# Mamba block: the residual rows added on TensorE with the identity, copied out by ScalarE

## The reference, cut to what matters

```
xz = einsum('bld,ed->ble', layernorm(x), in_proj_w)       # 256 -> 2 x 512: x part and gate z
u  = silu(causal_conv(x part))                            # 4 taps per channel
B, C, dt = split(u @ x_proj_w.T);  delta = softplus(dt @ dt_proj_w.T + dt_proj_b)
h_t = exp(delta_t * A) * h_{t-1} + delta_t * u_t * B_t    # 512 channels x 16 states
y   = (sum over states of h * C + D * u) * silu(z)
x   = x + y @ out_proj_w.T                                # out projection and residual
```

## Time and profile before

| | |
|---|---|
| Median of 3 runs | 3361.07 us (3359.82 to 3366.82) |
| Profiled execution, its own time | 3362.63 us |
| Its span, first to last instruction | 3360.8 us |
| Busy over the span | TensorE 2712.3 (81%), VectorE 2302.4 (69%), GpSimd 2124.2 (63%), ScalarE 1717.8 (51%) |
| Mean granted clock of TensorE | 0.906 |
| Mamba stage | from 0 to some 1815 us |

### The profile page before, as it was taken

One profiled execution on the slowest core, in us unless ns is written; L12 is line 12 of the kernel. 1 busy time (PEld: TensorE's weight loads), 2 busy tenths in 40 slices (PEclk: granted clock), 3 DMA queues, 4 the chain that ended last, 5 costly groups with the idle time before them and its releaser, 6 DMA issues.

```text
span 3360.8 us, 54089 instructions
## 1 busy us (share of the span) xinstructions
PE 2712.3 (81%) x20202; PEld 1495.0 (44%) x20202; DVE 2302.4 (69%) x2483; ACT 1717.8 (51%) x3115; POOL 2124.2 (63%) x1317
## 2 busy tenths in 40 slices
PE   5787788887888778887754499996999999359998
PEld 2233334333343333343332266554666666235665
DVE  1799999999999999999996522213666666552211
ACT  3677777777777777777751122223444443122221
POOL 1899999999999999999992054433333232124442
PEclk9899999988999889998876699998999999679999
DMA  3456565565566655666542033332111111213442
GB/s 112 103 127 155 137 144 133 140 145 140 140 138 146 146 134 132 144 149 143 133 107 60 13 90 71 83 51 59 46 46 40 52 46 38 67 28 87 89 89 25
DMA packets 227392, 330.01 MB, mean 98 GB/s; under 512 B 40546, under 2 KB 116834, under 8 KB 227011
## 3 DMA queue, kind: packets, MB, share of 16 engines
q1 hardware_dynamic: 202562, 292.49, 35.3%
q0 software_dynamic: 24576, 34.10, 6.0%
HBM read 240.52 MB, written 85.98 MB: 97 GB/s over the span
## 4 chain that ended last, share of the span: by engine, by line
PE 40%; POOL 24%; DVE 23%; issue 8%; ACT 3%; DMA 1%; SPq 0%; DVEq 0%; POOLq 0%; ACTq 0%
POOL m_side L584 14%; DVE m_pair L668 8%; POOL m_hc L593 7%; PE g_h L1341 6%; PE f_h L1341 6%; PE t_wb L2056 6%; DVE m_hc L668 5%; PE f_yp L1355 3%; PE m_wk L771 3%; PE g_yp L1355 3%; DVE m_hc L677 2%; PE t_num L2056 2%; PE m_y L863 2%; PE m_pair L919 2%; DVE t_am L1978 2%
## 5 line engine op out<-in xcount | busy, mean ns | idle before, releaser
L584 POOL TENSOR_TENSOR m_side<-m_du_r,m_bc 128x1024 f32<-128x1024 f32 x416 | 975.0, 2368 | 13.4 <-DMA m_du_r<-ddd 13.1
L351 ACT ACTIVATE m_pair<-m_delta_r,m_a_neg 128x512 f32<-128x512 f32 x832 | 539.7, 681 | 179.0 <-DVE m_hc L677 128.6
L593 POOL TENSOR_TENSOR m_hc<-m_hc,m_bc 128x1024 f32<-128x1024 f32 x208 | 492.2, 2370 | 99.6 <-DVE m_hc L668 97.9
L668 DVE TENSOR_TENSOR_SCAN m_pair<-m_pair,m_side 128x1024 f32<-128x1024 f32 x240 | 547.9, 2283 | 3.4 <-ACT m_pair L351 2.8
L863 PE MATMUL m_y<-m_hc,m_fold 128*32 128x512 f32 x2048 | 321.5, 702 | 229.8 <-DVE m_hc L677 121.2
L668 DVE TENSOR_TENSOR_SCAN m_hc<-m_pair,m_side 128x1024 f32<-128x1024 f32 x176 | 397.7, 2275 | 28.6 <-ACT m_pair L351 28.6
L677 DVE TENSOR_TENSOR m_hc<-m_pair,m_bc 128x1024 f32<-128x1024 f32 x304 | 370.5, 1219 | 7.3
L771 PE MATMUL m_wk<-m_xnT,m_w_in 128*128 128x512 f32 x512 | 276.9, 668 | 10.8 <-DVE m_cw_diag L725 10.0
L771 PE MATMUL m_wk<-m_xs,m_cw_diag 128*128 128x512 f32 x512 | 244.1, 605 | 15.5 <-ACT m_xs L416 15.5
L919 PE MATMUL m_pair<-m_b_diag,m_du_t 128*32 128x128 f32 x6144 | 203.8, 289 | 43.5 <-DVE m_hc L668 24.3
L919 PEld LDWEIGHTS m_pair<-m_b_diag,m_du_t 128*32 128x32 f32 x6144 | 179.0, 117 | 124.7 <-issue 123.4
(11 more groups left out here) (308 smaller groups left out, 4887.4 us busy)
## 6 DMA issues: line engine op xcount, KB each, us to landing
m_delta_r<-ddd SPq DMA_DIRECT2D x256, 256.0 KB, 6.8
m_du_r<-ddd SPq DMA_DIRECT2D x256, 256.0 KB, 7.7
m_bc<-bcd SPq DMA_DIRECT2D x256, 128.0 KB, 2.9
ddd<-m_delta SPq DMA_DIRECT2D x32, 512.0 KB, 3.2
ddd<-m_du SPq DMA_DIRECT2D x32, 512.0 KB, 4.1
f_w<-in_w SPq DMA_DIRECT2D x24, 512.0 KB, 6.1
g_w<-in_w SPq DMA_DIRECT2D x24, 512.0 KB, 6.1
m_xt<-in_x SPq DMA_DIRECT2D x16, 512.0 KB, 10.9
```

Of the source, the lines that this page charges most:

```text
L351: last = nc.scalar.activation(to, delta_r[:, c % 2, q, :], ACT.Exp, scale=a_neg[:, c * NQ + q, st:st + 1])
L584: nc.gpsimd.tensor_tensor(side[:, un % RING, :, :], du_r[:, c % 2, 2 * h:2 * h + 2, :], bc[:, 0, st:st + 1, :].to_broadcast([P, 2, T]), AL ...
L593: nc.gpsimd.tensor_tensor(hc[:, un % RING, :, :], hc[:, un % RING, :, :], bc[:, 1, st:st + 1, :].to_broadcast([P, 2, T]), ALU.mult).then_i ...
L668: nc.vector.tensor_tensor_scan(to, decay, added, 0.0, ALU.mult, ALU.add).then_inc(S["scan"], 1)
```

## The change

The two residual additions on VectorE are gone. TensorE adds the residual rows in the bank itself: behind the four matmuls of each 128 tokens it issues a fifth, with the identity as the stationary matrix and the loaded rows `xr` as the moving one, into the same accumulation; it waits for the load of these rows. ScalarE copies each half from the bank into `x1t` (the new `x1_out`, in its units 10 and 11, behind the fourth `cv_out` and ahead of the Silus). VectorE's statistics move from units 9 and 10 to 11 and 12, the aggregations from 10 to 12.

```diff
 # ScalarE
+            def x1_out(b, half):
+                act.wait_ge(S["op"], b * 2 + half + 1)
+                two = slice(half * 2, half * 2 + 2)
+                nc.scalar.copy(x1t[:, two, :], wk[:, half, :].rearrange("p (j c) -> p j c", c=C)).then_inc(S["x1"], 1)
...
                     if un == 7:
                         dut_out(b, 2)
+                    if post and un in (10, 11):
+                        x1_out(b - 1, (10, 11).index(un))
                     if un == 11:
                         if prep:
                             silu_u(b + 1, 1 - par)
...
             def epilogue():
+                x1_out(NB - 1, 0)
+                x1_out(NB - 1, 1)
                 out_norm3(NB - 1, 0)
 # VectorE
-            def residual(b, half):
-                dve.wait_ge(S["op"], b * 2 + half + 1)
-                if half == 0:
-                    dve.wait_ge(S["ld_xr"], b * 16 + 16)
-                two = slice(half * 2, half * 2 + 2)
-                nc.vector.tensor_tensor(x1t[:, two, :], wk[:, half, :].rearrange("p (j c) -> p j c", c=C), xr[:, two, :],
-                                        ALU.add).then_inc(S["x1"], 1)
...
-                        if un in (8, 10):
-                            residual(b - 1, (8, 10).index(un))
-                        if un in (9, 10):
-                            out_norm1(b - 1, (9, 10).index(un))
-                        if un == 10:
+                        if un in (11, 12):
+                            out_norm1(b - 1, (11, 12).index(un))
+                        if un == 12:
                             out_norm2(b - 1)
...
                 for half in range(2):
-                    residual(NB - 1, half)
                     out_norm1(NB - 1, half)
 # TensorE, outp
+                wait_alone(pe, S["ld_xr"], b * 16 + 16, S["tick"])
                 for jj in range(2):
                     j = half * 2 + jj
                     for k in range(KD):
-                        last = mm(wk[:, half, jj * C:(jj + 1) * C], yg[:, k, j * P:(j + 1) * P], w_out[:, k, :],
-                                  k == 0, k == KD - 1)
+                        mm(wk[:, half, jj * C:(jj + 1) * C], yg[:, k, j * P:(j + 1) * P], w_out[:, k, :],
+                           k == 0, False)
+                    last = mm(wk[:, half, jj * C:(jj + 1) * C], ident[:], xr[:, j, :], False, True)
                 last.then_inc(S["op"], 1)
```

## The result

The changed kernel takes 3432.8 us (median of 4 runs, 3431.4 to 3439.1) against 3361.8 of before: a ratio of 1.0212, interval [1.0196, 1.0228], 71 us slower. The forecast was 3429. The profiled execution took 3431.4, its span 3429.6.

A forecast was written before the change was run, and what follows sets the result against it. VectorE was taken as the bound, busy 102.6 of 105.9 us per Mamba batch, GpSimd 4 us behind. 14 x 4.69 = 65.7 us plus 2.0 in the epilogue, 67.7 in all, gave 3429 us; range 3393 to 3460.

The forecast's parts named there:

- A half of the out projection with the identity, start to start: On TensorE, the identity adds four records of 0.2156 us, so a half grows by 0.86 us from 3.45.
- Wait of the second copy: ScalarE's second copy, in unit 11 ahead of the Silus, waits about 3 us for TensorE in 14 batches.
- Wait ahead of unit 10's product: VectorE waits some 4 us for TensorE's sum ahead of unit 10's product with C.
- Wait ahead of scan 12: VectorE waits some 2 us for ScalarE's exponentials of unit 12; scan 12 starts 3.49 us later.
- Batches 1 to 14: Each steady Mamba batch loses 4.69 us, 65.7 us in all.
- Batch 15: No next batch, both out projection halves run in one go: put at 0, with 2 us to either side.
- Epilogue: Nothing is hidden: eight more records cost 2.4 us, copies for additions give 0.1 back; 2.0 us.
- hidden: Rival: second half ready when ScalarE comes to it, only removed VectorE work counts, 28 us off: 3337 us; 7 in 100.
- moved statistics: The second half's statistics and the aggregations stand behind scan 12, where VectorE has no gap: another 1.20 us per batch.
- TensorE's clock: Rival: clock falls in unit 15's longer wait, 0 to 2 us more per batch, at the top 3457 us; 15 in 100.
- A part covered: Rival: earlier out projection or statistics in a gap, a batch loses some 2 to 3.5 us: 3398 us; 11 in 100.

The follow-up runs named there:

- e1: The changed kernel with ScalarE's second copy in unit 12, behind the Silu block and unit 12's exponentials: 3405.5 us, 1.0124 against the kernel before.
- e2: The changed kernel without the identity matmuls, the residual left out of x: 3405.5 us, 1.0131 against the kernel before.
- e3: As e1, with TensorE issuing the out projection's second half in unit 9, behind the sum for unit 10's product: 3380.2 us, 1.0052.
- e5: Changed kernel, identity and ScalarE copy for the first half only, out projection halves in units 8 and 9, VectorE's second addition in unit 11: 3359.5 us, 0.9996.
- e9: As e7, with ScalarE's copy of the x projection behind unit 13's exponentials: 3365.8 us, 1.0010.
- e4: The kernel before with the identity matmuls on TensorE, VectorE copying each half out where it added: 3389.8 us, 1.0081.
- e7: TensorE's order as e5, identity for both halves, ScalarE copies in units 11 and 12, second half's statistics from the bank: 3366.4 us, 1.0020.
- e8: As e5, with ScalarE's copy of the x projection behind unit 13's exponentials: 3359.0 us, 0.9990.
- e6: The kernel before, out projection halves in units 8 and 9, both residual additions, statistics and aggregations in VectorE's unit 11: 3359.9 us, 0.9993.
- e10 to e12: Zero matmuls in TensorE's waits, added to e8, to the kernel before and to e6: 3366.0, 3370.4 and 3367.7 us.

## Why the prediction was right

From scan 8 to scan 13, where the change acts, mechanism and size were right, step by step; that the sum over the stage fits as well is in part luck. "Predicted" is the prediction's clock, as a distance from scan 8 (972.22).

| Step | Predicted | Measured |
|---|---|---|
| A half of the out projection with the identity, start to start | 3.45 + 0.86 = 4.31 us | 1002.67 to 1006.99: 4.32 |
| Wait of the second copy | about 3 us | 3.06 |
| Wait ahead of unit 10's product | some 4 us | 4.75 |
| Wait ahead of scan 12 | some 2 us | 1.97 |
| Scan 8 to scan 12 | 18.50 us | 18.56 |
| Scan 8 to scan 13 | 21.90 us | 21.94 |
| Batches 1 to 14 | 14 x 4.69 = 65.7 us | 66.6 |
| Batch 15 | 0, within 2 us | -1.5 |
| Epilogue | 2.0 us | 1.5 |

The measured 66.6 and -1.5 come from the distances of the Silus: the first 14 add up to 1485.2 us before and 1551.8 after, the last is 102.9 before and 101.4 after.

The luck is behind scan 13. The prediction let everything there move along unchanged, and it didn't: the softplus wait fell by 5.1 us and the wait ahead of scan 2 by 1.1, while the wait for TensorE's products at scan 22 grew by 4.4 (300 to 1700 us). These terms, which the sum had at nothing, nearly cancel. One reading mixes two ends: the sum that unit 10's product needs starts at 980.63 before and was put at about 983.4, which is where it ends; the wait that follows from it was right. Two sums are a little off: 0.9 us in each of 14 batches are 12.6 us to either side, not 14 to 15, and the 3337 of "hidden" counts from the profiled 3362.6, the forecast from the median.

The terms were also tested one by one. Of the growth from scan 8 to scan 13, 4.73 us here, e1 (no wait in front of the Silus) leaves 2.67 where 2.5 was expected, e2 (no identity) 3.00 for 3.0, and e3 (neither wait makes scan 12 late) 1.09 for 1.15. The 1.20 us of moved statistics, which looked like a detail, are what is left then.

Of the rivals, "hidden" fell with the 3.06 us wait, and e5 to e9 show more than that: where the waits are taken away, the work that VectorE is spared is worth no more than 0.2%. So its price of 28 us, 1.87 us per batch counted in full since VectorE is the busiest engine, was too high; the prediction's own rows have ScalarE's exponentials only 0.84 us ahead of scan 12. "TensorE's clock" did not come about where it was looked for: the wait at unit 15 grew from 1.30 to 2.72 us, and behind it 64 records take 1.95 us, as before. It came about ahead of scan 22, in four batches, for 6.6 us against 2.2. "A part covered" came about only in the waits behind scan 13: from scan 8 to scan 13 e1 to e4 found each term on the path.

Where the saving goes is shown in part. In e5, e7, e8 and e9 scan 12 comes 13.98 or 13.99 us behind scan 8, however much VectorE is spared, and in all 14 batches of each it starts 0.03 us behind the end of ScalarE's exponentials of unit 12 (981.71 + 1.30 and 983.04 in e5; 0.84 us in the kernel before). So ScalarE sets scan 12 there: in e7 VectorE comes 0.69 us before it and waits, in e5 at the same time. By scan 14 most of the 1.0 us is gone into waits for ScalarE's exponentials, behind copies that wait for TensorE: 0.2 us are left in e5 and 0.4 in e8. It isn't shown why those are not seen in the batch's length either. These are the distances between the gate's Silus from the tenth to the fourteenth, in us:

```
before  105.85 105.81 105.84 105.82 105.82
e5      105.82 105.81 105.82 105.80 106.10
e6      105.79 105.98 105.74 105.77 105.78
e7      105.84 105.84 105.82 105.81 105.82
e8      105.47 105.60 105.30 105.67 106.46
e9      105.72 105.88 105.72 105.71 105.90
```

Kernels with different work on VectorE, ScalarE and TensorE run at the same 105.8 us; e8 swings more, with a mean of 105.7. VectorE's own work alone would not give that; e10 to e12, whose filling made a half-speed stretch of its own, neither showed TensorE's clock to be the cause nor excluded it.

## What to carry to other kernels

A copy that waits holds up everything behind it in its queue: before moving work to a less busy engine, look at what stands behind its new place, and how long what it waits for runs. Count both sides of a wait: here the same late matmuls held ScalarE through a copy and VectorE through a sum, and only the later of the two was visible. And the time of the busiest engine is worth its full price only if no chain through the others is nearly as long; here ScalarE's exponentials were 0.84 us ahead of VectorE, and taking more than 1.0 us off VectorE ahead of them only made it wait.

## What the runs showed of the hardware

An fp32 matmul with the identity as the stationary matrix runs like any other: two records for 256 columns, spaced by 0.216 us, though one record by itself is shown with 0.38 us. TensorE's granted clock stayed at its upper level through a wait of 2.72 us (64 records in 1.95 us behind it) and was at its lower one behind a wait of 4.38 us. The length of the last wait doesn't decide it alone: in another batch the changed kernel ran at 0.53 from 1385.70 us on, one microsecond of full-speed matmuls behind a wait of 1.92 us.
